# Cross-attention and feed-forward layer on one core: the front ordered anew, first statistics of two batches on VectorE, row scales on GpSimd

## The chip, the cores and the metric

The kernel runs on one core of one Trainium2 chip. The metric is the device time of one execution in microseconds (us), the median of three runs. Five instruction streams work side by side: TensorE (PE), VectorE (DVE), ScalarE (ACT), GpSimd (POOL) and SyncE (SP), which here issues the transfers. Each runs its own list in order; they meet only through semaphores.

## The reference

`x` is 4 batches of 512 tokens with 512 features. Two layers follow each other:

```python
x = x + xattn(layernorm(x), fside, ctx)      # per batch b
x = x + ffn(layernorm(x), gate_w, w1, b1, w2, b2)

def smooth_quant_linear(x, w):               # twice per batch: c = 1 with fside, c = 2 with ctx
    s = sqrt(max(amax(|x|, axis=0), EPS) / max(amax(|w|, axis=0), EPS))
    xs, ws = x / s, w * s
    x_scale = max(rowmax(|xs|), EPS) / 127
    w_scale = max(rowmax(|ws|), EPS) / 127
    return round(xs / x_scale) @ round(ws / w_scale).T * x_scale * w_scale.T

def xattn(x, w1, w2):
    gate, up = split(smooth_quant_linear(x, w1))
    return smooth_quant_linear(silu(gate) * up, w2)

def ffn(x, ...):                             # 2048 tokens together
    logits = x @ gate_w.T                    # 8 experts
    sel = top_k(logits.sum(over tokens), 2)  # two experts for all tokens
    rw = softmax(logits[:, sel])
    return sum_k rw_k * (gelu(x @ w1[sel_k] + b1[sel_k]) @ w2[sel_k] + b2[sel_k])
```

Which two experts are taken is known only when all tokens of all four batches are normalised for the second time. So no weight of an expert can be loaded before the front is nearly done.

## The kernel before, in words

The program has two parts. The **front** (everything up to the choice of the experts) works on four batches b = 0 to 3, each through two quantised products c = 1 and 2. The **main part** runs 16 pairs of 256 hidden features (the function `pair`, the first of them `first_pair`) through TensorE and is left as it is but for one router product and the place of some semaphore increments.

A batch goes through the front like this; the names are those of the code. `moments` gives mean and variance of its tokens; `inv_std` on GpSimd gives the inverse deviation; `normalise` on ScalarE writes the normalised batch; `normed` on TensorE transposes it into PSUM, and `amax_x` on VectorE takes the largest values of the columns (`raw_weight` and `amax_w`, `raw_context` and `amax_c` do it for the weights). `ratio_x`, `root` and `inverse` make the smoothing vector, `smooth_rows` spreads it over rows, `smooth_x` and `smooth_weight` multiply with it. Then come the **scales of rows**: the maximum of each row (`abs_max`), a clip and a factor (`scale`, one small tensor_scalar, 128x4), and a reciprocal (`rscale`); before the change `row_scales` did all three on VectorE. `round_x` (ScalarE) and `round_weight` (GpSimd) round with them, TensorE transposes the rounded values (`rounded_x`, `rounded_w`), ScalarE casts them to bf16 (`integers_x`, `integers_w`), TensorE multiplies (`product`), and VectorE multiplies the scales back in (`dequant`). Between the products stand `gate`, `gate_up_product` and `ratio_a`. After the second product `add_residual` updates `res`, and the second normalisation (`moments(b, 2)`, `inv_std(b, 2)`, `normalise(b, 2)`, `normed2`) feeds the router: `token_sums`, `token_total`, `expert_sums`, `choose_experts`, then the load of the first expert weights.

Nothing orders this work but five lists of calls, written out by hand, one for each engine, and the table `SLOT_USES`, which says in which order four PSUM slots of two banks are used. A TensorE step that fills a slot waits until the step before it in that slot's list is drained. A wait placed early in a list holds all that stands behind it on that engine.

At the start SP issues the transfers in this order: the gate weights, the biases, x0, x1, w0, x2, w1, x3, w2, w3 and then the four contexts (x and w are 1 MB each, a context is 0.5 MB). VectorE's first real work is `amax_w(0, 0)`; the first moments of all four batches are ScalarE's, the second ones VectorE's.

## Time and profile before

| | us |
|---|---|
| median of the runs | 832.31 (three runs: 832.25, 832.31, 834.96) |
| the profiled execution | 837.12 |
| its span, first to last instruction | 835.3 |
| TensorE busy | 776.2 (93%) |
| VectorE busy | 494.4 (59%) |
| GpSimd busy | 437.3 (52%) |
| ScalarE busy | 363.1 (43%) |

The profile's first page gives these sums for the whole span. Since front and main part differ, the stretches have to be read apart: in the first 160 us VectorE is the fullest engine, after it TensorE is. The granted clock of TensorE was 0.97 of full on average. Times of single instructions come from the one profiled execution, which took 4.8 us more than the median of the unprofiled runs.

### The profile page before, as it was taken

To read this page: it belongs to the slowest core of one execution; us is meant where nothing else is said; L and a number is where in the kernel's file an instruction comes from. 1 tells how busy PE (TensorE), PEld (TensorE's weight loads), DVE (VectorE), ACT (ScalarE), POOL (GpSimd) and SP (SyncE) were. 2 spreads that over 40 slices of the span, in tenths; PEclk is the share of its full clock that TensorE was granted. 3 is DMA by queue.
4 is the path that set the end of the run, shared out by engine and by line. 5 is a ranking of instruction groups with operands and counts; after the bars stand their busy time and mean duration, and the time that the engine had idled before them with its cause. 6 is when DMAs were issued, how large, how long until landed. Compare 5 with 4: busy or idle time off the path is not lost.

```text
span 835.3 us, 11356 instructions
## 1 busy us (share of the span) xinstructions
PE 776.2 (93%) x3577; PEld 627.6 (75%) x3577; DVE 494.4 (59%) x699; ACT 363.1 (43%) x682; POOL 437.3 (52%) x453
## 2 busy tenths in 40 slices
PE   3587775699999999999999999999999999999998
PEld 3476553478788888888888888888888888888886
DVE  2899998879764545454545454545454545454545
ACT  7965666845533333333333343434343424342422
POOL 1467887155655555555555555545454546364622
PEclk9889898699999999999999999999999999999999
DMA  8500000120101010101010101000000000000022
GB/s 337 171 1 1 0 1 1 51 75 1 51 1 51 1 51 0 50 0 51 0 50 2 49 12 38 22 28 25 25 25 25 25 25 25 25 25 25 0 92 111
DMA packets 19078, 32.35 MB, mean 39 GB/s; under 512 B 872, under 2 KB 11240, under 8 KB 18160
## 3 DMA queue, kind: packets, MB, share of 16 engines
q1 hardware_dynamic: 19056, 32.07, 10.8%
q8 instruction: 12, 0.20, 0.1%
q14 instruction: 10, 0.08, 0.0%
HBM read 27.87 MB, written 4.19 MB: 38 GB/s over the span
## 4 chain that ended last, share of the span: by engine, by line
PE 81%; DVE 12%; issue 2%; DMA 2%; ACT 1%; POOL 1%; SPq 0%; DVEq 0%; POOLq 0%; ACTq 0%
PE slot L746 41%; PE slot L733 33%; DVE rmax L1154 3%; PE slot L791 3%; DVE xf L1204 2%; DMA wv<-in_fside_BxS2xS 2%; DVE peak_x L1154 2%; DVE xf L1217 1%; PE slot L607 1%; DVE wv L1217 1%; DVE stats L1145 1%; PE slot L596 1%; DVE scale L1195 1%; POOL h_lo L416 1%; DVE peak_a L1154 1%
## 5 line engine op out<-in xcount | busy, mean ns | idle before, releaser
L733 PE MATMUL slot<-xo,a_hi 128*128 128x512 f32 x840 | 258.9, 389 | 0.0
L1445 DVE SCALAR_TENSOR_TENSOR res<-slot,rw,res 128x512 f32<-128x512 f32 x256 | 179.5, 750 | 131.1 <-PE slot L746 130.2
L1474 DVE TENSOR_TENSOR e<-slot,e 128x512 f32<-128x512 f32 x150 | 103.8, 692 | 171.7 <-PE slot L733 171.7
L746 PE MATMUL slot<-w_hi,h_hi 128*128 128x512 f32 x512 | 201.1, 393 | 0.4 <-POOL h_lo L416 0.4
L746 PE MATMUL slot<-w_lo,h_hi 128*128 128x512 f32 x512 | 199.5, 390 | 0.0
L746 PE MATMUL slot<-w_hi,h_lo 128*128 128x512 f32 x512 | 199.2, 389 | 0.0
L733 PEld LDWEIGHTS slot<-xo,a_hi 128*128 128x128 f32 x840 | 157.3, 188 | 33.4 <-DVE e L1474 0.2
L416 POOL TENSOR_TENSOR h_lo<-e,h_hi 128x512 fp32r<-128x512 f32 x96 | 138.0, 1450 | 57.2 <-ACT e L1030 56.2
L733 PE MATMUL slot<-xo,a_lo 128*128 128x512 f32 x420 | 163.5, 389 | 0.0
L746 PEld LDWEIGHTS slot<-w_hi,h_hi 128*128 128x128 f32 x512 | 96.1, 188 | 25.3 <-POOL h_lo L416 5.6
L746 PEld LDWEIGHTS slot<-w_hi,h_lo 128*128 128x128 f32 x512 | 96.1, 188 | 20.2
L746 PEld LDWEIGHTS slot<-w_lo,h_hi 128*128 128x128 f32 x512 | 96.1, 188 | 19.4
L416 POOL TENSOR_TENSOR h_lo<-hid,h_hi 128x512 fp32r<-128x512 f32 x32 | 44.1, 1379 | 123.5 <-ACT hid L1030 123.5
L733 PEld LDWEIGHTS slot<-xo,a_lo 128*128 128x128 f32 x420 | 78.8, 188 | 16.6
L1029 ACT ACTIVATE h_hi<-e,b_now 128x512 fp32r<-128x512 f32 x90 | 64.9, 722 | 58.1 <-DVE e L1474 57.7
L1070 ACT COPY e<-slot 128x512 f32<-128x512 f32 x30 | 17.6, 586 | 164.5 <-PE slot L733 164.5
L430 POOL TENSOR_TENSOR a_lo<-raw,a_hi 128x256 fp32r<-128x256 f32 x45 | 34.3, 762 | 96.0 <-ACT a_hi L923 96.0
L926 ACT CAST w_hi<-raw 128x512 fp32r<-128x512 f32 x32 | 19.8, 622 | 110.0 <-PE slot L746 110.0
L435 POOL TENSOR_TENSOR w_lo<-raw,w_hi 128x512 fp32r<-128x512 f32 x30 | 38.7, 1290 | 50.5 <-ACT w_hi L926 50.5
L1030 ACT ACTIVATE e<-e,b_now 128x512 f32<-128x512 f32 x90 | 63.8, 708 | 0.0
L1029 ACT ACTIVATE h_hi<-slot,b_now 128x512 fp32r<-128x512 f32 x38 | 26.2, 689 | 67.8 <-PE slot L733 56.6
L430 POOL TENSOR_TENSOR a_lo<-ssum,a_hi 128x256 fp32r<-128x256 f32 x60 | 43.9, 741 | 0.0
(144 smaller groups left out, 834.1 us busy)
## 6 DMA issues: line engine op xcount, KB each, us to landing
raw<-in_L_ffn_w SPq DMA_DIRECT2D x32, 512.0 KB, 3.3
res<-in_x SPq DMA_DIRECT2D x4, 1024.0 KB, 9.7
wv<-in_fside_BxS2xS SPq DMA_DIRECT2D x4, 1024.0 KB, 14.9
out_x<-res SPq DMA_DIRECT2D x3, 1024.0 KB, 3.9
cv<-in_ctx SPq DMA_DIRECT2D x4, 512.0 KB, 11.0
out_x<-res SPq DMA_DIRECT2D x4, 256.0 KB, 2.7
b_row<-in_L_ffn_b SPq DMA_DIRECT2D x2, 256.0 KB, 4.3
b_rows<-in_L_ffn_b SPq DMA_DIRECT2D x1, 64.0 KB, 1.9
```

Source lines behind the costliest of these rows:

```text
L416: g.tensor_tensor(h_lo[:, i, :], hid[i][:, :], h_hi[:, i, :].bitcast(F32), ALU.subtract).then_inc(h_ready, 1)
L430: g.tensor_tensor(a_lo[:, i, :, :], A_OF[i], a_hi[:, i, :, :].bitcast(F32), ALU.subtract).then_inc(a_ops_ready, 1)
L435: g.tensor_tensor(w2_lo[:, f, :], raw2[:, f, :], w2_hi[:, f, :].bitcast(F32), ALU.subtract).then_inc(w2_ready, 1)
L733: last = t.matmul(dst, a[:, i, k, :], xo[tp][:, v, k, :], start=(start and n == 0), stop=(n == 3 * H - 1), skip_group_check=True)
L746: last = t.matmul(y_bank[j][:, :], a[:, i, j * P:(j + 1) * P], v[:, f, :], start=(start and n == 0), stop=(not start and n == 2), skip_gro ...
L791: last = t.matmul(TILE_BANK[n], a[:, 2 * f + h, k, :], xo[q][:, v, k, :], start=(m == 0), stop=(m == 3 * KD - 1))
L926: s.copy(w2_hi[:, f, :], raw2[:, f, :]).then_inc(w2_hi_ready, 1)
L1029: s.activation(h_hi[:, i, :], src, ACT.Gelu_apprx_tanh, bias=bias).then_inc(hid_ready, 1)
L1030: s.activation(hid[i][:, :], src, ACT.Gelu_apprx_tanh, bias=bias).then_inc(hid_ready, 1)
L1154: return v.tensor_reduce(dst, src, AX.X, ALU.max, apply_absolute_value=True)
L1445: v.scalar_tensor_tensor(out=r, in0=y_bank[j][:, :], scalar=rw[:, ds(p, 1), n:n + 1].rearrange("p a b -> p (a b)"), in1=r, op0=ALU.mult, o ...
L1474: v.tensor_tensor(dst[:, :], src, other[:, :], ALU.add).then_inc(comb_ready, 1)
```

## The change

- SP issues the transfers in the order x0, w0, x1, w1, c0, x2, w2, c1, x3, w3, c2, c3. The gate weights and biases are issued by ScalarE.
- The first moments of batches 0 and 1 go to VectorE, ahead of and between its first maxima. Those of batches 2 and 3 stay on ScalarE.
- The second moments of batch 0 go from VectorE to ScalarE. The second normalisation of batch 2 goes from ScalarE to GpSimd.
- `row_scales` is split in three: `row_max` on VectorE, `row_scale` on GpSimd (the small tensor_scalar, 16 in all), `row_inverse` on VectorE, which waits for GpSimd. The three stand at different places of their lists, with other work between them.
- All five lists and `SLOT_USES` are written in a new order. The router products stand as 0, sums, 1, 2, 3, with none left inside the first pair; before they stood as sums, 0, 1, 2, and the fourth after the first tile of the first pair.

```diff
-            sp.dma_start(gw_rows, gate_w).then_inc(gw_load, 16)
-            sp.dma_start(b1_rows[:, :], b1_v).then_inc(b1_load, 16)
...
             load_x(0)
+            load_w(0)
             load_x(1)
-            load_w(0)
+            load_w(1)
+            load_c(0)
             load_x(2)
-            load_w(1)
+            load_w(2)
+            load_c(1)
             load_x(3)
-            load_w(2)
             load_w(3)
...
+            def row_scale(b, c, w):
+                pool.wait_ge(rmax_done, ROW_MAXIMA.index("xw"[w] + f"{c}.{b}") + 1)
+                g.tensor_scalar(scale[b][:, w, :], rmax[b][:, w, :], QEPS, 1.0 / QMAX, ALU.max, ALU.mult
+                                ).then_inc(scale_done, 1)
+
...
+            def normalise(b):
+                pool.wait_ge(nmr_ready[b], 2)
+                for j in range(TT):
+                    g.tensor_scalar(xv[b][:, j, :], res[:, b * TT + j, :], rstd[1][b][:, j:j + 1], nmr[1][b][:, j:j + 1],
+                                    ALU.mult, ALU.add).then_inc(xn2_ready[b], 1)
...
+            router(0)
             expert_sums()
-            router(0)
             router(1)
             router(2)
+            router(3)
...
-                    if tp == 0:
-                        router(3)
...
-            def row_scales(b, m, w, ready):
-                link(abs_max(rmax[b][:, w, :], m))
-                link(v.tensor_scalar(scale[b][:, w, :], rmax[b][:, w, :], QEPS, 1.0 / QMAX, ALU.max, ALU.mult))
-                v.reciprocal(rscale[b][:, w, :], scale[b][:, w, :]).then_inc(ready[b], 1)
+            def row_max(b, m, w):
+                abs_max(rmax[b][:, w, :], m).then_inc(rmax_done, 1)
+
+            def row_inverse(b, c, w):
+                dve.wait_ge(scale_done, SCALES.index("xw"[w] + f"{c}.{b}") + 1)
+                v.reciprocal(rscale[b][:, w, :], scale[b][:, w, :]).then_inc((xscale_ready, wscale_ready)[w][b], 1)
```

The two places where the order matters most for what follows. First VectorE at the very start; peak_x0 are the column maxima of batch 0 (its input and its weight), stats1 the first statistics of batch 1. Before:

```order
L1154 TENSOR_REDUCE peak_x0<-slot3 128x2
L1154 TENSOR_REDUCE peak_x0<-slot2 128x2
L1154 TENSOR_REDUCE peak_x1<-slot2 128x2
L1154 TENSOR_REDUCE peak_x1<-slot3 128x2
L1154 TENSOR_REDUCE peak_x0<-slot3 128x2
L1154 TENSOR_REDUCE peak_x0<-slot2 128x2
L1169 TENSOR_SCALAR clip0<-peak_x0 128x8
```

The same place now, up to the same clip0:

```order
L1183 BN_STATS stats0<-res 128x6 x4
L1186 BN_AGGR mv0<-stats0 128x2 x4
L1192 TENSOR_REDUCE peak_x0<-slot0 128x2
L1183 BN_STATS stats1<-res 128x6 x4
L1186 BN_AGGR mv1<-stats1 128x2 x4
L1188 TENSOR_SCALAR nmean1_1<-mv1 128x4
L1189 TENSOR_SCALAR var_e1_1<-mv1 128x4
L1192 TENSOR_REDUCE peak_x0<-slot2 128x2
L1192 TENSOR_REDUCE peak_x0<-slot0 128x2
L1192 TENSOR_REDUCE peak_x1<-slot1 128x2
...
L1207 TENSOR_SCALAR clip0<-peak_x0 128x8
```

Two statistics have moved in between the same six maxima; both wait for a transfer of x. The second place is GpSimd's list in the first product; wv0 is the weight of batch 0, multiplied with its smoothing row (L342 before, L348 now) and rounded (L348 before, L354 now). Before:

```order
L342 TENSOR_TENSOR wv0<-wv0,xf0 128x512 x4
L327 TENSOR_TENSOR rstd1_2<-var_e1_2,neg_half 128x4
L330 TENSOR_TENSOR nmr1_2<-nmean1_2,rstd1_2 128x4
L336 TENSOR_TENSOR sroot1<-ratio1,half 128x4
L348 TENSOR_SCALAR wv0<-wv0,rscale0 128x512 x4
L342 TENSOR_TENSOR wv1<-wv1,xf0 128x512 x4
L336 TENSOR_TENSOR sroot2<-ratio2,half 128x4
L348 TENSOR_SCALAR wv1<-wv1,rscale1 128x512 x4
```

Now:

```order
L348 TENSOR_TENSOR wv0<-wv0,xf0 128x512 x4
L359 TENSOR_SCALAR scale0<-rmax0 128x4
L333 TENSOR_TENSOR rstd1_3<-var_e1_3,neg_half 128x4
L336 TENSOR_TENSOR nmr1_3<-nmean1_3,rstd1_3 128x4
L359 TENSOR_SCALAR scale0<-rmax0 128x4
L354 TENSOR_SCALAR wv0<-wv0,rscale0 128x512 x4
L348 TENSOR_TENSOR wv1<-wv1,xf0 128x512 x4
L342 TENSOR_TENSOR sroot2<-ratio2,half 128x4
L359 TENSOR_SCALAR scale1<-rmax1 128x4
L348 TENSOR_TENSOR wv2<-wv2,xf0 128x512 x4
L359 TENSOR_SCALAR scale1<-rmax1 128x4
L354 TENSOR_SCALAR wv1<-wv1,rscale1 128x512 x4
```

Each small scale stands between the large pieces and behind four of them in two cases, and the rounding that waits for it stands later in the same list.

## Rows read from the trace of the kernel before

**Rows 1.** The page: the chain that ended last, shares by engine

```profile
PE 81%; DVE 12%; issue 2%; DMA 2%; ACT 1%; POOL 1%; SPq 0%; DVEq 0%; POOLq 0%; ACTq 0%
```

**Rows 2.** Who TensorE waited for, from 168 to 300 us: total, times, longest

```profile
PE slot L746 <- POOL h_lo L416: 0.4, 1, 0.4
```

**Rows 3.** Stretches: length, each engine's busy time (x instructions), PEclk, DMA share, GB/s

```profile
120.00:130.00 10.00, 5.59 (x37) 4.61 (x36) 6.41 (x14) 8.68 (x18) 4.99 (x9) 0.84 0.00 1
140.00:150.00 10.00, 2.99 (x20) 2.04 (x20) 9.90 (x18) 7.20 (x14) 6.30 (x5) 0.87 0.01 2
150.00:160.00 10.00, 7.14 (x32) 5.66 (x32) 7.68 (x16) 7.89 (x16) 2.40 (x4) 0.61 0.00 0
260.00:300.00 40.00, 40.00 (x177) 32.84 (x176) 20.23 (x28) 14.82 (x28) 21.25 (x21) 1.00 0.08 27
```

**Rows 4.** Stretches, VectorE alone: length, busy (x instructions), PEclk, DMA share, GB/s

```profile
0.00:26.30 26.30, 7.93 (x10) 1.00 0.93 345
26.30:142.60 116.30, 109.48 (x167) 0.85 0.04 14
142.60:161.90 19.30, 16.83 (x35) 0.71 0.00 1
```

**Rows 5.** Timeline of the start: start, length, engine, line [idle before <-releaser]

```profile
0.74 0.41 SPq L251 DMA_DIRECT2D wsc_row<-in_L_ffn_gate_w  x1
1.63 0.89 SPq L255 DMA_DIRECT2D res<-in_x  x2
6.92 0.63 ACT L846 ACTIVATE xf<-res 128x512 f32<-128x512 f32 x1 [3.98 <-DMA res<-in_x]
12.61 3.65 PE L508 MATMUL slot<-ident,wv 128*128 128x128 f32 x16 [8.94 <-DMA wv<-in_fside_BxS2xS]
17.72 3.63 PE L508 MATMUL slot<-ident,wv 128*128 128x128 f32 x16 [1.46 <-DMA wv<-in_fside_BxS2xS]
28.30 3.46 DVE L1154 TENSOR_REDUCE peak_x<-slot 128x2 f32<-128x1024 f32 x3
```

**Rows 6.** Timeline, VectorE: one `moments` of four pieces, first and last row

```profile
111.18 2.46 DVE L1145 BATCH_NORM_STATS2 stats<-res 128x6 f32<-128x512 f32 x4
114.16 0.16 DVE L1151 TENSOR_SCALAR var_e<-mv 128x4 f32<-128x4 f32 x1
```

**Rows 7.** Groups, 0 to 170 us: busy us, mean ns of one, idle before

```profile
L1195 DVE TENSOR_SCALAR scale<-rmax 128x4 f32<-128x4 f32 x16 | 7.4, 462 | 0.6
```

**Rows 8.** VectorE's scale operation: ns min/median/max

```profile
L1195 DVE TENSOR_SCALAR scale<-rmax x16: 170/281/1843, 38.7 to 132.8; 128x4 f32<-128x4 f32 x16
```

**Rows 9.** Groups of GpSimd, 0 to 160 us: busy us, mean ns, idle before

```profile
L342 POOL TENSOR_TENSOR wv<-wv,xf 128x512 f32<-128x512 f32 x16 | 19.9, 1281 | 5.5 <-ACT xf L865 5.5
L348 POOL TENSOR_SCALAR wv<-wv,rscale 128x512 f32<-128x512 f32 x16 | 10.8, 693 | 6.7 <-DVE rscale L1196 6.7
L327 POOL TENSOR_TENSOR rstd<-var_e,neg_half 128x4 f32<-128x4 f32 x8 | 9.0, 1126 | 25.1 <-ACT var_e L854 18.6 <-DVE var_e L1151 6.6
L348 POOL TENSOR_SCALAR cv<-cv,rscale 128x256 f32<-128x256 f32 x16 | 7.4, 482 | 1.3 <-DVE rscale L1196 1.3
```

**Rows 10.** Timeline of the tail, TensorE, VectorE and ScalarE

```profile
142.60 3.32 DVE L1264 TENSOR_TENSOR res<-res,wv 128x512 f32<-128x512 f32 x2
142.62 1.97 PE L596 MATMUL slot<-ident,xf 128*128 128x128 f32 x16 [1.57 <-DVE wv L1217]
151.36 7.17 PE L596 MATMUL slot<-ident,xf 128*128 128x128 f32 x32 [6.77 <-ACT xf L833]
161.06 7.26 PE L607 MATMUL slot<-xo,gwt 128*16 128x512 f32 x24
161.73 0.16 DVE L1283 FIND_INDEX8 top_i<-top_v,sum_row 128x8 uint32<-128x8 f32 x1
166.56 1.32 ACT L920 CAST a_hi<-raw 128x256 fp32r<-128x256 f32 x4
168.16 0.62 PE L791 MATMUL slot<-xo,a_hi 128*128 128x512 f32 x2
```

More of the change, by code:

```diff
@@ L366, in _ @@
             root(0, 1)
+            root(1, 1)
+            inv_std(2, 1)
+            smooth_weight(0, 1)
+            row_scale(0, 1, 0)
             inv_std(3, 1)
-            smooth_weight(0, 1)
-            inv_std(2, 1)
-            root(1, 1)
+            row_scale(0, 1, 1)
             round_weight(0, 1)
@@ L1325, in _ @@
             dve.sem_inc(y_free, TT)
+            dve.sem_inc(comb_ready, 15)
+            dve.sem_inc(h_ready, 4)
+            moments(0, 1)
             amax_w(0, 0)
+            moments(1, 1)
             amax_w(0, 1)
+            amax_x(0, 0)
             amax_w(1, 0)
+            amax_x(0, 1)
             amax_w(1, 1)
[L1330 to L1331 removed]
             ratio_x(0)
@@ L1334, in _ @@
             inverse(0, 1)
-            amax_w(2, 0)
-            amax_w(3, 0)
             amax_x(1, 1)
             ratio_x(1)
+            amax_c(0)
             smooth_x(0, 1)
+            inverse(1, 1)
+            scale_x(0, 1)
+            amax_w(3, 0)
+            amax_w(2, 0)
             scale_w(0, 1)
+            amax_w(3, 1)
+            row_inverse(0, 1, 1)
+            row_inverse(0, 1, 0)
             amax_w(2, 1)
-            amax_w(3, 1)
-            inverse(1, 1)
-            amax_c(1)
+            smooth_x(1, 1)
@@ L1345, in _ @@
             amax_x(2, 0)
-            amax_c(0)
-            smooth_x(1, 1)
             amax_x(2, 1)
             ratio_x(2)
+            scale_x(1, 1)
+            inverse(2, 1)
+            amax_x(3, 0)
             scale_w(1, 1)
+            amax_x(3, 1)
+            row_inverse(1, 1, 0)
+            smooth_x(2, 1)
+            ratio_x(3)
+            row_inverse(1, 1, 1)
+            scale_w(2, 1)
             dequant(0, 1, 0)
-            inverse(2, 1)
+            scale_x(2, 1)
+            inverse(3, 1)
@@ L1353, in _ @@
             dequant(0, 1, 1)
-            amax_x(3, 0)
-            smooth_x(2, 1)
-            amax_x(3, 1)
-            ratio_x(3)
-            scale_w(2, 1)
-            ratio_a(0)
-            inverse(3, 1)
-            dequant(1, 1, 0)
-            inverse(0, 2)
-            dequant(1, 1, 1)
-            smooth_x(3, 1)
-            smooth_x(0, 2)
-            scale_w(0, 2)
-            scale_w(3, 1)
-            ratio_a(1)
+            row_inverse(2, 1, 0)
+            row_inverse(2, 1, 1)
@@ L1369, in _ @@
+            amax_c(1)
+            smooth_x(3, 1)
+            scale_x(3, 1)
+            dequant(1, 1, 0)
+            ratio_a(0)
+            dequant(1, 1, 1)
+            scale_w(3, 1)
+            row_inverse(3, 1, 0)
+            amax_c(2)
+            row_inverse(3, 1, 1)
+            inverse(0, 2)
             dequant(2, 1, 0)
             dequant(2, 1, 1)
+            smooth_x(0, 2)
+            ratio_a(1)
+            scale_x(0, 2)
+            scale_w(0, 2)
             inverse(1, 2)
-            amax_c(2)
+            row_inverse(0, 2, 0)
@@ L1373, in _ @@
+            amax_c(3)
+            row_inverse(0, 2, 1)
+            dequant(3, 1, 0)
             smooth_x(1, 2)
-            dequant(0, 2, 0)
-            scale_w(1, 2)
-            dequant(0, 2, 1)
-            dequant(3, 1, 0)
             ratio_a(2)
             dequant(3, 1, 1)
-            moments(0, 2)
-            inverse(2, 2)
-            dequant(1, 2, 0)
-            amax_c(3)
-            smooth_x(2, 2)
-            scale_w(2, 2)
-            ratio_a(3)
-            inverse(3, 2)
+            scale_x(1, 2)
@@ new lines, in _ @@
+            scale_w(1, 2)
+            row_inverse(1, 2, 0)
+            dequant(0, 2, 0)
+            row_inverse(1, 2, 1)
+            inverse(2, 2)
+            ratio_a(3)
+            smooth_x(2, 2)
+            scale_x(2, 2)
+            inverse(3, 2)
+            row_inverse(2, 2, 0)
+            dequant(0, 2, 1)
+            scale_w(2, 2)
+            smooth_x(3, 2)
+            scale_x(3, 2)
+            row_inverse(2, 2, 1)
+            dequant(1, 2, 0)
+            scale_w(3, 2)
+            row_inverse(3, 2, 0)
@@ L1388, in _ @@
             dequant(1, 2, 1)
-            smooth_x(3, 2)
-            scale_w(3, 2)
+            row_inverse(3, 2, 1)
             dequant(2, 2, 0)
+            dequant(2, 2, 1)
             moments(1, 2)
-            dequant(2, 2, 1)
             dequant(3, 2, 0)
             dequant(3, 2, 1)
+            moments(2, 2)
             add_last_residual()
-            moments(2, 2)
             moments(3, 2)
             keep_lo(0, 0)
+            keep_lo(1, 0)
             normalise_last()
+            token_sums(2)
```

290 lines of the change are left out of this document (156 added, 134 removed), and 16 rows, old and new, of the table SLOT_USES.

## The prediction

> **What bounds the kernel now.** I read the chain that ended last first: TensorE holds 81% of it [rows 1]. Then I asked who TensorE waits for once the main part runs: from 168 to 300 us there is a single wait of 0.4 us [rows 2], and the stretch 260 to 300 is busy for 40.00 of 40 us [rows 3]. So from its first tile, at 168.16 us [rows 10], TensorE runs without a gap. The main part is hardly changed and can't get shorter. What the change is worth is by how much earlier that stream starts, plus what is taken out of it.
>
> In the front the reader is to see VectorE. From the clip of batch 0 (26.30) to the end of the last `dequant`, where the last residual starts (142.60 [rows 10]), it is busy for 109.5 of 116.3 us; before that for 7.9 of 26.3 us, behind it for 16.8 of 19.3 us [rows 4]. It is the full engine of the middle; in the first 26 us it waits for transfers and transposes; behind 142.60 a chain runs over four engines up to the choice of the experts at 161.73 [rows 10]. I take the four stretches one by one.
>
> **A, the start, up to the clip of batch 0: 26.30 before.** x0 is there at 6.92, w0 at 12.61, w1 at 17.72 [rows 5]. The step from 6.92 to 12.61 is x1 and w0, 5.7 us. In the new order w0 and x1 follow x0, so x1 lands where w0 did, at 12.6. SP no longer issues two small loads first, which took 0.9 us (0.74 to 1.63 [rows 5]); they now run beside the large ones, so I count 0.6 of it: 12.0. VectorE then needs one `moments`, 111.18 to 114.32, 3.1 us [rows 6], and five of the six maxima, 3.46/3 = 1.15 each [rows 5], 5.8 us. The other `moments` and the first maximum fit between x0 and x1. The clip comes at 12.0 + 3.1 + 5.8 = 20.9. A is 5.4 us shorter, and two `moments`, 6.1 us of new VectorE work lie in time that was idle. Bounds: if x1 came only at 14.8, one transfer of half that 5.7 later, the gain is 26.30 - 23.7 = 2.6; with the full 0.9 and no gap, 6.2.
>
> **B, the middle, 116.3 us before.** Removed from VectorE: 16 scale operations, 7.4 us [rows 7]; the median is 281 ns and the longest 1843 [rows 8], and the long ones stood beside GpSimd's work. Each also had a link on either side, for which I estimate 0.1 us, 1.6 in all. The second moments of batch 0 leave too: 3.1 [rows 6]. Together 12.1 us. Added to GpSimd: 16 tensor_scalars of 128x4, which the trace does not show there. Its tensor_scalar took 693 ns with 512 elements and 482 with 256 [rows 9], which leaves 0.27 for almost none; the upper end is its power on 128x4, 1.13 us [rows 9]. I take 0.27, since the operation is of the first kind: 4.3 us. If GpSimd stood in the way with all of it at 1.13, it were 18.
>
> What hides these 4.3 us is VectorE's other work between `row_max` and `row_inverse`: in the first product a maximum of 1.15 us or more stands there. Queued behind a waiting `row_inverse` on VectorE are `dequant` and `smooth_x`; ScalarE's and GpSimd's rounding waits for it. In the second product the cover is thin: maxima are half as long, GpSimd has the weights of ctx, the gated products and the residuals to do, and `scale_w` of batches 2 and 3 waits for it. I laid the new lists out in time, every instruction starting when its list and its semaphores let it, with its duration from the rows. VectorE's larger waits there are 1.0 us before a `dequant(3,1)`, 1.2 before the row maxima of the ctx weight of batch 2, 2.1 before `dequant(2,2)` and 0.5 twice elsewhere; with small ones 8.0 us, against the 6.8 that it idles now (116.30 - 109.48 [rows 4], more than half of it in 120 to 130 [rows 3]). In it the two small operations of the moments of batch 1 also stand 2.5 us behind GpSimd's residuals. So of the 12.1 us the 1.6 of links were idle anyway; busy time falls by 10.5 - 2.5 = 8.0, idle time rises by 1.2, and B comes out 6.8, say 7 us, shorter. The old lists, laid out in the same way, come within 1.1 us of the trace at 160 us, so I trust the layout to 2 or 3 us. Bounds: 0, if the waits eat everything, and 12.1, if none is added.
>
> A rule speaks against B. The Trainium skill (SBUF — State Buffer, "SBUF: two separate sides") says that VectorE and GpSimd share a port pair as an exclusive lock: a VectorE operation with two SBUF inputs or in a fast mode, and a GpSimd operation, block each other whole; Perfetto Trace Analysis, "Optimizing Scalar/DVE Operations", adds that moving work between those two might not help. By that rule the trace agrees as to the lock: the same 128x4 operation takes 170 to 1843 ns [rows 8]. The rule would leave the 16 operations their own 0.27 us on GpSimd but take VectorE's wait for the lock away, so it does not decide against the sum; what would is the first rival.
>
> **C, the tail, 19.3 us before.** Each tail has the same chain: residual, moments, inverse deviation, normalise, transposes, token sums. GpSimd normalises batch 2 with four tensor_scalars of 0.69 [rows 9], 2.8 us, and ScalarE spent 2.9 on it. One router product more now stands ahead of the sums. TensorE ran the first 16 transposes there in 1.97 us and the last 32 in 7.17 [rows 10], 0.12 against 0.22 each: its granted clock was 0.61 of full in 150 to 160, that is mostly the lower level of 1.2 GHz, after a stretch with 3 of 10 us busy [rows 3]. At that level eight router matmuls (24 took 7.26 [rows 10], 0.30 each) can delay the sums by up to 2.4; at the full one the layout hides them. I take C 1.5 longer; bounds 1 shorter and 5 longer.
>
> **D, from the choice to the dense stream, 6.4 us.** SyncE, the load, ScalarE's and VectorE's split of the weights stay; the router products 1, 2, 3 fill the time that 0, 1, 2 filled, so nothing moves. But the fourth product no longer stands in the dense stream: eight matmuls of 512 columns at 40.00/177 = 0.226 [rows 3], 1.8 us. Bounds 0 and 1.8.
>
> **The sum**: -5.4 - 7.0 + 1.5 - 1.8 = -12.7 us. The profiled execution took 837.12 us (span 835.3), so it would take 824.4; against the median of 832.31 it is **819.6 us**.
>
> **The rivals.** *First, GpSimd becomes the bound of the middle.* For it: in the second product it already holds most of its time, and 4.3 us come to it. Against: in 120 to 130 it was busy for 5.0 of 10 us [rows 3], and 12.1 us leave VectorE. B gives nothing: -5.4 + 1.5 - 1.8 = -5.7, 826.6 us.
>
> *Second, slower: the small scales queue behind GpSimd's large pieces.* The place is `row_scale` behind `smooth_weight` (four pieces of 1.28, 5.1 us [rows 9]), with `row_inverse` and all of VectorE standing behind it. For each of 16 scales w us of VectorE's time are lost beyond the layout; the point from which the kernel is slower by 4.2 is 16 w = 12.7 + 4.2, w = 1.06 us. With two pieces each (2.56) in half of the cases it is 20.5 us, 840.1 us. For it: VectorE is in order and the two engines are the fullest. Against: the scales stand ahead of the next large group in most places, and VectorE has 1.2 us or more to do meanwhile.
>
> *Third, the clock stays low through the tail.* 64 transposes of the second normalisation at 0.22 instead of 0.12 cost 6.4 us, of which the 32 that already ran so [rows 10] are in the time before: 3.2 more, 822.8 us. For it: TensorE is no busier in the new tail.
>
> *Fourth, the transfers don't come earlier* (A gives 2.6): 822.4 us. *Fifth, no waits are added in the middle*: B gives 12.1, 814.5 us. That the change does not do what it says has no room here: the operations are gone from VectorE's list.
>
> **How the numbers follow.** Forecast 0.50, GpSimd bound 0.13, scales queue 0.04, low clock 0.14, late transfers 0.09, no waits 0.10. The range runs from the fifth rival (814.5) to the first (826.6), 814 to 827; what it leaves out is the slower rival and some of each end. Half a per cent, 4.2 us, is about what a measurement of this kernel can tell from no change; faster means below 828.1. The forecast, the last three rivals (0.83) and half of the first are faster, 0.89; the other half, with a layout that was too kind by a few us, is the same, 0.07; slower 0.04.
>
> **What would show it.** A: the clip of batch 0 at 20.9 us and x1 landing near 12. B: the line of the scales on GpSimd at 0.27 us each and gone from VectorE, VectorE's last `dequant` ended near 130. C: the choice of the experts near 151 (161.73 - 10.9). D: TensorE's first tile near 157, no router product inside the first pair. The prediction is wrong if a scale on GpSimd takes about 1 us, if VectorE waits for `scale_done` for more than a few us in total, or if TensorE shows gaps behind its first tile.

## The result, and the profile after

| | median us | runs | lowest to highest |
|---|---|---|---|
| before | 833.26 | 4 | 832.25 to 834.96 |
| changed | 824.26 | 4 | 822.56 to 826.86 |

The ratio is 0.989 (95%: 0.986 to 0.993): 9.0 us faster, where 12.7 were forecast (819.6, range 814 to 827). Further runs, made beside the experiments below, give 835.3 to 835.8 for the kernel before (17, 23 and 11 runs in three groups) and 825.94 for the changed one (6 runs, beside the first group): 9.4 us there. One of the 23, at 867.68 us and a granted clock of 0.878, is a slow execution and left out of the ratios. I take the difference of the medians as 9.4.

The profiled execution of the changed kernel took 823.26 us (span 821.4). The main part first: the chain that ended last is again TensorE's (shares by engine).

```profile
PE 82%; DVE 9%; POOL 4%; issue 3%; DMA 1%; ACT 1%; ACTq 0%; DVEq 0%; POOLq 0%
```

VectorE's share fell by three points and GpSimd's rose by as many [rows 1]. Who TensorE waits for, from 150 to 300 us (total, times, longest):

```profile
PE slot L781 <- POOL h_lo L450: 0.4, 1, 0.4
PE slot L826 <- issue: 0.3, 1, 0.3
PE slot L641 <- DVE xo L1268: 0.2, 1, 0.2
```

As before [rows 2] there is nothing to gain there. From the first matmul with `w_hi` to the end the two spans have 653.1 and 653.0 us left, so the whole difference is made ahead of it. The stretches of VectorE by the same three moments as [rows 4] (length, then busy time of PE, PEld, DVE, ACT and POOL, granted clock, DMA share, GB/s):

```profile
0.00:21.44 21.44, 12.15 (x69) 10.10 (x69) 13.46 (x31) 8.52 (x14) 3.51 (x15) 1.00 0.94 347
21.44:130.59 109.15, 80.54 (x506) 59.67 (x512) 99.64 (x142) 82.17 (x161) 90.60 (x125) 0.90 0.08 30
130.59:150.13 19.54, 16.12 (x67) 11.02 (x68) 17.30 (x35) 14.27 (x28) 10.11 (x10) 0.57 0.00 1
```

The reader is to see three things. The start is 4.9 us shorter, and VectorE does 5.5 us more work in it. The middle is 7.1 shorter (116.26 to 109.15): VectorE's busy time falls by 9.8, and its idle time grows from 6.8 to 9.5. The tail, counted from the end of the last `dequant` (142.56 before) to the choice (161.73), is 0.4 longer, 19.5 against 19.2, and TensorE's granted clock in it is 0.57 of full. The start, in rows that answer to [rows 5] (start, length, engine, line):

```profile
1.36 0.36 ACTq L965 DMA_DIRECT2D b_rows<-in_L_ffn_b  x1
7.25 0.47 PE L523 MATMUL slot<-ident,b_rows 128*128 128x128 f32 x1 [3.40 <-DMA b_rows<-in_L_ffn_b]
8.39 2.46 DVE L1183 BATCH_NORM_STATS2 stats<-res 128x6 f32<-128x512 f32 x4
9.03 3.65 PE L542 MATMUL slot<-ident,wv 128*128 128x128 f32 x16 [1.31 <-DMA wv<-in_fside_BxS2xS]
12.58 2.46 DVE L1183 BATCH_NORM_STATS2 stats<-res 128x6 f32<-128x512 f32 x4
21.44 0.16 DVE L1207 TENSOR_SCALAR clip<-peak_x 128x8 f32<-128x8 f32 x1
```

Moving the two small loads to ScalarE's queue freed SyncE's, and x0 landed at 5.66 us and x1 at 11.40. But the biases came only at 7.2, and VectorE's first statistics stand behind the copy of what they feed, so they began at 8.39 though x0 had been there for 2.7 us. The groups of the scales (busy us, mean ns, idle before), where [rows 7] had 7.4 us on VectorE:

```profile
L359 POOL TENSOR_SCALAR scale<-rmax 128x4 f32<-128x4 f32 x16 | 3.7, 233 | 7.8 <-DVE rmax L1192 6.8
L1236 DVE RECIPROCAL rscale<-scale 128x4 f32<-128x4 f32 x16 | 2.5, 167 | 0.6 <-POOL scale L359 0.5
```

A scale costs GpSimd 233 ns, and VectorE waits for all sixteen for 0.5 us in total. VectorE's longer waits in the middle (21.4 to 130.6):

```profile
DVE wv L1260 <- PE slot L609: 3.4, 1, 3.4
DVE rmax L1192 <- POOL cv L348: 2.0, 2, 1.4
DVE xf L1249 <- ACT xf L901: 1.0, 1, 1.0
```

The wait of 1.4 is for the ctx weight of batch 2, the place that the prediction named with 1.2. The end of the middle and the tail, in time, from the timelines of all engines:

```profile
119.72 2.73 DVE L1260 SCALAR_TENSOR_TENSOR wv<-slot,scale,wsc_row 128x512 f32<-128x512 f32 x4 [3.40 <-PE slot L609]
121.74 7.42 POOL L373 TENSOR_TENSOR res<-res,wv 128x512 f32<-128x512 f32 x6
125.43 1.31 DVE L1188 TENSOR_SCALAR nmean<-mv 128x4 f32<-128x4 f32 x1
126.65 1.31 DVE L1189 TENSOR_SCALAR var_e<-mv 128x4 f32<-128x4 f32 x1
135.52 4.09 POOL L378 TENSOR_SCALAR xf<-res,rstd,nmr 128x512 f32<-128x512 f32 x4
137.84 2.85 DVE L1268 TENSOR_TENSOR xo<-xf,xo 128x1024 fp32r<-128x1024 f32 x2
139.58 1.97 POOL L333 TENSOR_TENSOR rstd<-var_e,neg_half 128x4 f32<-128x4 f32 x1
142.82 3.87 PE L630 MATMUL slot<-ident,xf 128*128 128x128 f32 x16 [0.76 <-ACT xf L866]
146.34 2.48 PE L641 MATMUL slot<-xo,gwt 128*16 128x512 f32 x8
150.13 0.16 DVE L1326 FIND_INDEX8 top_i<-top_v,sum_row 128x8 uint32<-128x8 f32 x1
156.04 0.70 PE L826 MATMUL slot<-xo,a_hi 128*128 128x512 f32 x2 [0.26 <-issue]
```

The two small operations of the moments take 1.31 us each beside GpSimd's six residual additions; elsewhere they take 0.16 [rows 6]. GpSimd's four pieces of `normalise` take 4.09 us where I counted 2.8 (three take 0.77 and the last, beside `keep_lo`, 1.84), and its power 1.97 where the mean was 1.13 [rows 9]: the last piece and the power overlap VectorE's `keep_lo` (L1268), a subtraction of two SBUF operands. By the rule of the Trainium skill (SBUF — State Buffer, "SBUF: two separate sides") VectorE and GpSimd lock each other out there; the trace agrees, with these 1.84 and 1.97 us as the price for GpSimd.

### The profile page after: what moved, and what is told of

Read it like the earlier page. It is cut to its first block, busy times and chain, and to the rows that moved or that the text cites. A ratio compares the mean times of both kernels' runs of the same rounds, so it can differ in the third digit from the quotient of the medians.

```text
span 821.4 us, 11341 instructions
## 1 busy us (share of the span) xinstructions
PE 775.2 (94%) x3570; PEld 624.4 (76%) x3577; DVE 487.6 (59%) x693; ACT 355.2 (43%) x660; POOL 445.9 (54%) x473
## 4 chain that ended last, share of the span: by engine, by line
PE 82%; DVE 9%; POOL 4%; issue 3%; DMA 1%; ACT 1%; ACTq 0%; DVEq 0%; POOLq 0%
PE slot L781 42%; PE slot L768 34%; PE slot L826 3%; DVE rmax L1192 2%; DVE xf L1249 1%; DVE peak_x L1192 1%; POOL res L373 1%; DVE peak_a L1192 1%; DVE xf L1260 1%; DMA b_rows<-in_L_ffn_b 1%; POOL cv L348 1%; DVE stats L1183 1%; POOL rstd L333 1%; POOL h_lo L450 1%; PE slot L563 1%
## 5 line engine op out<-in xcount | busy, mean ns | idle before, releaser
L768 PEld LDWEIGHTS slot<-xo,a_hi 128*128 128x128 f32 x840 | 157.3, 188 | 33.4 <-DVE e L1542 0.2
L781 PEld LDWEIGHTS slot<-w_lo,h_hi 128*128 128x128 f32 x512 | 96.1, 188 | 19.5
## 6 DMA issues: line engine op xcount, KB each, us to landing
wv<-in_fside_BxS2xS SPq DMA_DIRECT2D x4, 1024.0 KB, 12.7
```

Of the source, the lines that this page charges most:

```text
L768: last = t.matmul(dst, a[:, i, k, :], xo[tp][:, v, k, :], start=(start and n == 0), stop=(n == 3 * H - 1), skip_group_check=True)
L781: last = t.matmul(y_bank[j][:, :], a[:, i, j * P:(j + 1) * P], v[:, f, :], start=(start and n == 0), stop=(not start and n == 2), skip_gro ...
```

## The experiments

Each kernel is compared with runs of the kernel before on the same chip in the same minutes, and the ratios are to these. Their median is 835.3 us beside the first four that follow here (changed again, new lists with the scales on VectorE, new lists with the old transfers, router product back), 835.8 beside the next four (before again, old lists with the scales on GpSimd, old lists with the new transfers, small loads on SyncE) and 835.4 beside the last four. Where a difference to the changed kernel is given, it is to its repetition, 825.94, which ran beside the first group only. How far such differences can be trusted is seen from two sets of one program: the kernel before gave 833.76 as an experiment (12 runs) and 835.8 beside it (23 runs), and the changed kernel 824.26 and 825.94. A difference of about 2 us between two kernels is therefore not told from this scatter by its median alone. Moments are read from each trace: the clip of batch 0, the end of the last `dequant`, the choice of the experts, TensorE's first tile with `a_hi`.

| kernel | median us | ratio to before, 95% | clip | dequant | choice | tile |
|---|---|---|---|---|---|---|
| before, again | 833.76 | 0.998, 0.996 to 1.000 | 25.6 | 141.3 | 158.7 | 164.6 |
| changed, again | 825.94 | 0.989, 0.986 to 0.992 | 21.3 | 132.4 | 152.5 | 158.4 |
| new lists, scales on VectorE | 828.23 | 0.992, 0.989 to 0.994 | 21.8 | 137.5 | 157.3 | 163.2 |
| new lists, old transfers | 833.59 | 0.998, 0.996 to 0.999 | 24.1 | 142.8 | 163.0 | 168.9 |
| router product back | 827.88 | 0.992, 0.989 to 0.994 | 21.6 | 132.4 | 151.5 | 157.3 |
| old lists, scales on GpSimd | 848.28 | 1.015, 1.013 to 1.017 | 26.1 | 155.7 | 173.1 | 179.1 |
| old lists, new transfers | 836.26 | 1.001, 0.999 to 1.003 | 24.6 | 143.4 | 160.8 | 166.8 |
| small loads on SyncE | 826.16 | 0.988, 0.986 to 0.990 | 22.0 | 132.7 | 153.0 | 158.9 |
| statistics on ScalarE | 829.26 | 0.992, 0.990 to 0.994 | 26.9 | 136.0 | 155.0 | 160.9 |
| filler transposes | 824.56 | 0.987, 0.984 to 0.989 | 22.2 | 131.5 | 150.3 | 155.9 |
| tail reordered | 823.44 | 0.985, 0.982 to 0.987 | 21.9 | 131.5 | 150.5 | 156.2 |
| filler and reordered | 824.97 | 0.987, 0.985 to 0.989 | 21.6 | 133.6 | 152.6 | 158.3 |

**The changed kernel once more.** No edit.

> The changed kernel once more, unaltered: the control of the other three, and a second trace of the same program. If the executions of one program differ by where TensorE's clock falls in the front (theory), its first dense tile will not start at 156.0 us as in the first trace but up to 2 us off, with other stretches at the lower clock, and the main part will take the same 665 us. If they differ in the main part instead (rival), the first tile starts within 0.3 us of 156.0 and the end moves. Time 822 to 827.

825.94 us (824.53 to 827.1). The trace differs from the first one by 2.3 us at the first tile and by 0.0 from the first matmul with `w_hi` on (653.01 and 653.03). More than half of the difference, 1.3 us, comes at one place of the middle (about 0.5 lies ahead of it and 0.5 in the tail):

```profile
125.94 3.76 DVE L1188 TENSOR_SCALAR nmean<-mv 128x4 f32<-128x4 f32 x1
129.68 2.71 DVE L1260 SCALAR_TENSOR_TENSOR wv<-slot,scale,wsc_row 128x512 f32<-128x512 f32 x4
```

The operation of 0.16 us took 3.76 here, and `dequant` behind it began 1.8 us later than in the first trace. GpSimd at that time, same trace:

```profile
122.25 7.43 POOL L373 TENSOR_TENSOR res<-res,wv 128x512 f32<-128x512 f32 x6
129.85 1.02 POOL L333 TENSOR_TENSOR rstd<-var_e,neg_half 128x4 f32<-128x4 f32 x1 [0.17 <-DVE var_e L1189]
```

The small operation ended when the six additions of 1.24 us each ended: it stood behind three of them in a row. In the first trace it began just as far into the six additions (3.69 us after their start in both) and took 1.31, as the operation behind it did. What decides between the two cases is not shown. Of the nine traces with the new lists and the scales on GpSimd three show the long wait.

**The scales back on VectorE, new lists kept.**

```diff
-                abs_max(rmax[b][:, w, :], m).then_inc(rmax_done, 1)
+                link(abs_max(rmax[b][:, w, :], m))
+                v.tensor_scalar(scale[b][:, w, :], rmax[b][:, w, :], QEPS, 1.0 / QMAX, ALU.max, ALU.mult
+                                ).then_inc(scale_done, 1)
```

and GpSimd's 16 `row_scale` calls go.

> The changed kernel with the 16 scale operations back on VectorE, each straight behind its row maximum with a wait in between; all five lists otherwise as they are, GpSimd's 16 operations gone. Theory (VectorE sets the pace of the middle, and the operation costs it its own time, two links and the wait for the port that GpSimd holds): laid out in time the last dequant ends 6.6 us later and the first dense tile starts 6.7 us later: 830 to 832. Rival (the new order did it, the place of the scales is nothing, since they fit in waits): within 2 us of the changed kernel.

828.23: 2.3 us over the repetition of the changed kernel, less than I expected. The two sets do not overlap (827.67 to 831.4 against 824.53 to 827.1), but 2.3 us is hardly more than the scatter between sets of one program. Its profiled execution was the slowest of its runs (831.4), so the 5 us that its trace shows in the middle are too many. The operation itself:

```profile
L1212 DVE TENSOR_SCALAR scale<-rmax 128x4 f32<-128x4 f32 x16 | 9.2, 577 | 0.6
```

9.2 us leave VectorE when the scales go to GpSimd, and about 2.3 of them reach the end. The rest is lost on the way, in waits by my reading; no run separates them.

**The old transfers under the new lists.** Again small loads first on SyncE, then x0 x1 w0 x2 w1 x3 w2 w3 and ctx last.

```diff
+            sp.dma_start(gw_rows, gate_w).then_inc(gw_load, 16)
+            sp.dma_start(b1_rows[:, :], b1_v).then_inc(b1_load, 16)
-            load_w(0)
             load_x(1)
+            load_w(0)
...
-            act.dma_start(gw_rows, gate_w).then_inc(gw_load, 16)
-            act.dma_start(b1_rows[:, :], b1_v).then_inc(b1_load, 16)
```

> The changed kernel with the transfers in the old order (x0, x1, w0, x2, w1, x3, w2, w3, contexts) and the two small loads on SyncE in front of them again. Theory (stretch A is set by when w0, x1 and w1 land and carried to the end by a full VectorE): clip of batch 0 at about 23.3 instead of 21.4, and since w1 and the contexts come later than the new lists want them, the last dequant 6.6 us and the first dense tile 6.7 us later: 829 to 832. Rival (the start has slack; transfers are hidden anyway): under 2 us.

833.59: 7.7 us over the changed kernel, more than forecast. The clip is only 2.7 us later; the rest is lost behind it, where VectorE's list still asks for tiles in the order in which the new transfers would bring them. Who VectorE waits for, 0 to 143 us (the 4.1, the 3.6 and the 2.7 lie ahead of the clip, the 5.9 behind it, for the transposes of a normalised batch):

```profile
DVE peak_x L1190 <- PE slot L559: 5.9, 1, 5.9
DVE peak_x L1190 <- PE slot L542: 4.4, 2, 4.1
DVE gwt L1159 <- PE slot L523: 3.6, 1, 3.6
DVE stats L1181 <- DMA res<-in_x: 2.7, 1, 2.7
```

**The fourth router product back in the dense stream.**

```diff
-            router(3)
...
+                    if tp == 0:
+                        router(3)
```

> The changed kernel with the fourth router product and its copy back inside the first pair, behind the first tile. Theory: the first tile starts where it did (within 0.3 us), and the eight matmuls of 0.23 us come into the dense stream: 1.9 us slower. Rival (the wait for the first expert weights had no room, so taking the product out lets the first tile start sooner): no difference.

827.88, 1.9 us over the changed kernel, as expected by the median. The chain of waits of this kernel shows the product at its old place (start, length, what):

```profile
157.34 4.57 PE slot L825 x12
161.91 1.84 PE slot L641 x8
163.75 2.72 PE slot L825 x12
```

The product takes 1.84 us of the stream. But that is not all that this trace shows. Twelve matmuls ahead of it take 4.57 us and the twelve behind it 2.72: TensorE had idled 2.5 us before the first tile, and its granted clock from 157.3 to 162.0 us is 0.64. From the first tile to the first matmul with `w_hi` this kernel needs 15.8 us against 12.3, so 3.4 more, and its first tile is 1.0 us earlier than in the repetition. That the medians differ by just the price of the product is in part luck.

**The kernel before once more.** No edit.

> The kernel before, unaltered, for a second trace of it. Theory (the main part from the first down product takes 653.0 us in every execution, and what differs between executions of one program is the front, by where TensorE's clock falls): main part within 0.2 us of 653.1, the middle from the first clip to the last dequant 1 to 3 us shorter than the 116.3 of the first trace, since that execution was at the slow end of its runs. Rival: the same front, another main part.

833.76 (832.34 to 837.13). Its trace, from a run of 834.97, is nearer to the median than the one that I predicted from (837.12): its tail has the length 17.4 us instead of 19.2, at a granted clock of 0.80 instead of 0.71. Two things that I expected did not come: the middle is only 0.6 us shorter than in the first trace (1 to 3 expected), and from the first matmul with `w_hi` on it takes 654.4 us, not 653.1. TensorE's part of that is the same within 0.2 us; from the end of its last matmul to the end of the span it is 5.1 us against 3.9, and no engine works at its end: the last transfer of the output lands later. Its last transposes and its router products, to be held against 7.17 and 7.26 [rows 10]:

```profile
149.15 6.32 PE L596 MATMUL slot<-ident,xf 128*128 128x128 f32 x32 [5.84 <-ACT xf L833]
158.00 5.72 PE L607 MATMUL slot<-xo,gwt 128*16 128x512 f32 x24
```

VectorE's middle in this trace and in the repetition of the changed kernel (columns as above), and the sixteen scales in this one, to be held against 7.4 us [rows 7]:

```profile
25.64:141.29 115.65, 83.35 (x507) 63.15 (x512) 107.36 (x166) 78.54 (x146) 87.77 (x110) 0.85 0.05 16
21.32:132.40 111.08, 83.43 (x513) 59.35 (x512) 101.13 (x142) 83.47 (x163) 91.69 (x126) 0.88 0.08 30
L1195 DVE TENSOR_SCALAR scale<-rmax 128x4 f32<-128x4 f32 x16 | 6.0, 375 | 0.5
```

**The scales on GpSimd with the old lists.** On the kernel before: each `row_scale` stands behind the `smooth_weight` of its batch, the maxima and inverses stay where they are.

```diff
-                link(abs_max(rmax[b][:, w, :], m))
-                link(v.tensor_scalar(scale[b][:, w, :], rmax[b][:, w, :], QEPS, 1.0 / QMAX, ALU.max, ALU.mult))
+                abs_max(rmax[b][:, w, :], m).then_inc(rmax_done, 1)
+                scales[0] += 1
+                dve.wait_ge(scale_done, scales[0])
```

> The kernel before with nothing changed but the 16 scale operations: they are GpSimd's, behind the weight products of the same batch, and VectorE waits for each in place, its lists not rearranged. Theory (the move pays only because the new lists put other work between row maximum and inverse; in place, VectorE stands behind up to four products of 1.28 us): laid out in time the last dequant ends 8 to 9 us later and the first tile 7 to 9 us later, 842 to 845. Rival (the move itself is the gain): 2 to 7 us faster than before.

848.28, 12.5 us slower than before (ratio 1.015). VectorE's waits in the middle of this kernel, 26 to 155 us:

```profile
DVE rscale L1224 <- POOL scale L357: 8.5, 16, 1.5
DVE peak_a L1179 <- PE slot L609: 5.5, 2, 3.4
DVE xf L1232 <- ACT xf L890: 2.1, 3, 1.3
DVE smooth L1215 <- POOL sroot L340: 2.1, 1, 2.1
```

VectorE's busy time in the middle is 107.16 us against 109.48 [rows 4] and 107.36 in the second trace of before, but the stretch is 129.5 long against 116.3 and 115.7. Every one of the sixteen inverses waits for GpSimd, 0.53 us on average, and what follows each of them is late for TensorE and ScalarE. This is the mechanism of the second rival. At 0.53 us for each scale it costs half of what I had set as the point from which the changed kernel would be slower; here that is enough, since no reordered list gives anything back. So the move as placed here does not pay without the new lists, in which VectorE has a maximum or a `smooth_x` to do between a row maximum and its inverse. Only one placing in GpSimd's old list was run, behind the weight products; whether the scales ahead of these products would cost less was not tested. The Trainium skill (Perfetto Trace Analysis, "Optimizing Scalar/DVE Operations") says that moving work between these two engines might not help, because they share a port. The time agrees for the move alone; the waits above are for the moved operation itself, so they do not show that reason.

**The new transfers under the old lists.** On the kernel before, x0 w0 x1 w1 c0 x2 w2 c1 x3 w3 c2 c3; the small loads stay on SyncE.

```diff
             load_x(0)
-            load_x(1)
             load_w(0)
-            load_x(2)
+            load_x(1)
             load_w(1)
+            load_c(0)
+            load_x(2)
```

> The kernel before with nothing changed but the order of the large transfers, which is the new one (x0, w0, x1, w1, c0, x2, ...). Theory (transfers, moments and lists belong together: the first clip comes 0 to 1 us sooner since it stands behind ScalarE's two moments and w1, and batches 2 and 3 get their data later than the old lists want it): 0 to 3 us slower than before. Rival (the transfer order alone is stretch A's gain): 3 to 5 us faster, first clip near 22.

836.26 against 835.8: no difference (0.999 to 1.003). The clip is 1 to 1.7 us earlier than in the traces of before, and the gain is gone by the end of the `dequant`.

**The two small loads back on SyncE, ahead of the large ones.**

```diff
+            sp.dma_start(gw_rows, gate_w).then_inc(gw_load, 16)
+            sp.dma_start(b1_rows[:, :], b1_v).then_inc(b1_load, 16)
...
-            act.dma_start(gw_rows, gate_w).then_inc(gw_load, 16)
-            act.dma_start(b1_rows[:, :], b1_v).then_inc(b1_load, 16)
```

> The changed kernel with the gate weights and biases issued by SyncE in front of the large loads, as before, the new order of the large ones kept. In the changed kernel the biases landed at 7.2 us (3.2 before), and VectorE's first statistics, which stand behind them, began at 8.4 with x0 there at 5.7. Theory: they begin at about 6.9 now (x0 lands 0.9 us later), but the first clip hangs on x1 and w1 as well and comes 0 to 0.8 us sooner: 0 to 1 us faster than the changed kernel. Rival (the late biases cost the whole 1.5 us to the end): 1.5 us faster.

826.16, the same as the changed kernel. VectorE's start in this kernel:

```profile
6.64 2.48 DVE L1183 BATCH_NORM_STATS2 stats<-res 128x6 f32<-128x512 f32 x4 [2.29 <-DMA res<-in_x]
12.12 1.22 DVE L1192 TENSOR_REDUCE peak_x<-slot 128x2 f32<-128x1024 f32 x1 [2.32 <-PE slot L544]
```

The first statistics begin 1.7 us earlier than in the changed kernel, and the first maximum then waits 2.3 us for the transposes of w0, which is late by the small loads. Either order of the queues costs the same: mending the late biases in this way gains nothing.

**The first statistics of batches 0 and 1 on ScalarE again.** They are those of the first normalisation.

```diff
+            moments(0, 1)
+            moments(1, 1)
```

in ScalarE's list ahead of `normalise(0, 1)`, and gone from VectorE's.

> The changed kernel with the first moments of batches 0 and 1 back on ScalarE, ahead of its two first normalisations; transfers and all else as changed. Theory (stretch A: ScalarE needs 5.8 us for each of the two, one behind the other, and the first clip waits for them): laid out in time the first clip comes at 26.0 instead of 21.6 and the first dense tile 4.2 us later, 4 to 5 us slower than the changed kernel, about 830. Rival (the middle has slack that takes it up): under 2 us.

829.26, 3.3 us over the changed kernel, a little less than forecast. The clip comes at 26.9 us, 5.5 us later; at the end of the last `dequant` 3.6 to 5.4 of it are left (136.0 against 132.4 and 130.6).

**Filler transposes against the low clock.** 30, 12 and 12 transposes of the identity into a free bank, ahead of the last three batches of the second normalisation.

```diff
+            def busy_work(n):
+                emptied("y.0.0")
+                for _ in range(n):
+                    t.transpose(slot[0][:, 1, 0:P], ident[:, :], ident[:, :])
...
+                if h == 0 and b:
+                    busy_work((30, 12, 12)[b - 1])
```

> The changed kernel with 30, 12 and 12 transposes more on TensorE (of the identity into a bank that nobody uses then) ahead of the second normalisation's transposes of batches 1, 2 and 3, where TensorE idled 5.2, 1.7 and 0.8 us. They do nothing but keep TensorE at work. Theory (the tail is 2.7 us longer than the old one in good part because TensorE runs 14 to 17 us of it at the lower clock, after it has idled): the stretch from 130 to 147 shows the full clock, the last 16 transposes take 2.0 instead of 3.9 us, the choice of the experts comes 2 to 3 us sooner: 2 to 3 us faster than the changed kernel. Rival (the clock falls all the same, or the tail hangs on VectorE and GpSimd and not on TensorE): no gain, or up to 3 us slower for the added work.

824.56: 1.4 us under the repetition of the changed kernel and 0.3 over its first set (824.26), so no difference is shown. The stretch of the tail in the changed kernel (length, busy time of PE, PEld, DVE, ACT and POOL, granted clock, DMA share, GB/s):

```profile
130.00:140.00 10.00, 6.75 (x24) 4.06 (x25) 9.86 (x25) 6.41 (x13) 8.87 (x11) 0.51 0.01 2
```

The same stretch with the filler, and the first router product behind the last transposes, from this kernel's timeline:

```profile
130.00:140.00 10.00, 6.17 (x43) 4.33 (x41) 9.86 (x27) 6.29 (x13) 8.89 (x11) 1.00 0.00 0
146.21 2.02 PE L648 MATMUL slot<-xo,gwt 128*16 128x512 f32 x8
```

With the filler TensorE is at its full level of 2.4 GHz from 130 us to the first tile (1.00 instead of 0.51 in this stretch), and that router product takes 2.02 us instead of 2.48. Yet the tail is 18.7 us long against 19.5 and 20.1. By these traces the low clock costs about a microsecond there: up to 142.8 us the chain that ends last is VectorE's and GpSimd's, but for one ScalarE operation.

**The tail reordered on VectorE.** VectorE's part of the last normalisation goes ahead of two of the splits `keep_lo`, and the token sums of batch 2 ahead of one.

```diff
-            keep_lo(0, 0)
-            keep_lo(1, 0)
             normalise_last()
+            keep_lo(0, 0)
             token_sums(2)
             keep_lo(0, 1)
+            keep_lo(1, 0)
             keep_lo(1, 1)
```

> The changed kernel with the two subtractions for the low parts of batches 0 and 1 that stood between the last moments and the last normalisation on VectorE put behind the latter. In both traces of the changed kernel they held GpSimd's last two steps up: its normalisation piece took 1.84 us instead of 0.77 and the power behind it 1.97 instead of 1.01. Theory (this port conflict is 1 to 2 us of the longer tail): var_e to the last nmr takes 2.0 us instead of 3.9; part of it is lost again since the subtractions come later: laid out, 0 to 1.1 us faster. Rival (nothing of it reaches the end): same.

823.44 (822.19 to 824.17), 2.5 us under the repetition of the changed kernel and 0.8 under its first set, 0.985 of the time before: the lowest median of all. The trace shows less: its tail is 19.0 us against 19.5 and 20.1, so 0.5 to 1.1 us come from the reordered tail. It has the long wait of 3.76 us in the middle too, and its first tile (156.21) is no earlier than in the first trace of the changed kernel (156.04). Where the rest of the 2.5 comes from is open. GpSimd's part of the tail in this kernel, to be held against 4.09 and 1.97 above:

```profile
136.41 3.05 POOL L378 TENSOR_SCALAR xf<-res,rstd,nmr 128x512 f32<-128x512 f32 x4
139.43 1.00 POOL L333 TENSOR_TENSOR rstd<-var_e,neg_half 128x4 f32<-128x4 f32 x1
140.51 0.20 POOL L336 TENSOR_TENSOR nmr<-nmean,rstd 128x4 f32<-128x4 f32 x1
```

With no VectorE operation on two SBUF operands beside them, the four pieces take 1.0 us less and the power its usual 1.0.

**Both.** The filler and the reordered tail.

> Both of the last two edits. Theory: they add up, 2 to 4 us faster than the changed kernel, 822 to 824. Rival: the router products and the load of the first expert weights set the first tile, and all that is won before the choice is lost behind it: the same as the better of the two.

824.97: the two do not add up. The trace has the small operation's delay in the middle again (`dequant` ends at 133.6), and a tail of 19.0 us, as with the reordering alone. Whether the filler itself costs something in the middle stays open; the intervals of these last kernels overlap.

## Why the prediction was right in kind and 3.3 us too good

The sum by its four terms, once from the two traces first shown, and once from the two traces nearest to the medians (before again, 834.97 us; changed again, 825.67):

| term | forecast | first pair | pair near the medians |
|---|---|---|---|
| A, start to the clip | -5.4 | -4.9 | -4.3 |
| B, clip to the last `dequant` | -7.0 | -7.1 | -4.6 |
| C, to the choice | +1.5 | +0.4 | +2.7 |
| D, to the first tile | 0 | -0.5 | -0.1 |
| D, router product and the rest behind the tile | -1.8 | -1.9 | -3.2 |
| sum | -12.7 | -14.0 | -9.5 |

**The bound was read rightly.** TensorE's stream is as long as before but for the router product, and everything moved with its start. No gap came behind the first tile but the 0.4 us that stood there before. Between the traces nearest to the medians the three terms of the front come to 6.2 us, where the forecast had 10.9; the last row hides a part of that.

**A** held, 0.5 to 1.1 us short. x1 landed at 11.4, as worked out (12.0). What I had not seen is that the biases, now in ScalarE's queue, would land 4 us later than before, and that VectorE's first statistics stand behind them. The small loads put back on SyncE's queue give nothing. The two statistics moved into the idle start were worth 3.3 us by themselves.

**B is the term that fell shortest of the medians**: 4.6 us, where 7.0 were forecast. Its working is there. In the first pair VectorE's busy time fell by 9.8 us (8.0 forecast) and its idle time rose by 2.7 (1.2), the scale takes 233 ns on GpSimd (270), and two of the named waits are there, for the ctx weight 1.4 us, and behind GpSimd's residuals, where the two small operations take 2.3 more than alone. The other wait of 3.4 us, for `dequant(2,2)` behind TensorE, is longer than the 2.1 laid out. Between the traces near the medians, though, busy time fell by only 6.2 us, and idle time rose by 1.7. Two terms that I set as fixed vary between executions. The sixteen scales cost 7.4 us in the trace that I predicted from and 6.0 in the second trace of the same program (7.7 with the old lists and new transfers). And the wait of the two small operations behind GpSimd, set at 2.5 us, is 2.3 or 3.6 between two runs of one program. Together that is about the 2.4 us that are missing; smaller differences go both ways. It is not one place alone: with the router product back both small operations took 1.31 us and the middle was still 110.8 us long.

**C** ran short by 1.2 us against the medians. The layout had the tail from 19.3 up by 1.5, that is 20.8. The new tail is 19.0 to 20.3 us in the traces with the new lists (18.7 with the filler), so it came out 0.5 to 1.8 shorter than laid out. What was mis-sized more is the tail before: three of four traces with the old lists have one of 17.4 us, and the trace that I predicted from had 19.2, in an execution at the slow end of its kernel. Of these 1.8 us, 0.9 are the last residual on VectorE (3.32 us [rows 10] against 2.38) and 0.9 the last 32 transposes (7.17 against 6.32).

**The yardstick** joins B and C: I took the difference to an execution of 837.12 us and set it against a median of 832.31. The tail of 19.2 us was that execution's own, and its scales cost 1.4 us more than in the second trace of the same program. The first pair sets it against an execution of 823.26, below the median of its kernel; that B agrees with the forecast to 0.1 us in it is in part luck.

**D** held in the product: it takes 1.84 us of the stream where it is put back (1.8 forecast), and from the first tile to the first matmul with `w_hi` the changed kernel needs 12.3 us against 14.1. In the pair near the medians the row shows 3.2, of which 1.4 lie behind the first matmul with `w_hi`, mostly in the last transfer of the output, which the change does not touch.

**The rivals.** Three of them gave a time nearer to the measured 824.26 than the forecast did: GpSimd as the bound of the middle (826.6), the low clock (822.8) and late transfers (822.4). None of the three mechanisms is there at its price. GpSimd is not the bound: B is 4.6 to 7.1 us and not nothing. Scales that queue behind large pieces are real, but only with the old lists: 12.5 us slower. The low clock was there (0.57 in the tail) and costs about 1 us by the filler's traces, not 3.2. Late transfers: refuted by the landing of x1 (11.4, not 14.8). No added waits: refuted, idle time rose by 1.7 to 2.7 us.

**The parts are not a sum.** Taken from the changed kernel one at a time, the transfers are worth 7.7 us, the statistics 3.3, the scales 2.3 and the router product 1.9, together 15 where the whole is 9.4. The last two are about as large as the scatter between sets of one program. Put alone into the kernel before, the transfers give 0 and the scales cost 12.5. The second moments of batch 0 on ScalarE, the second normalisation of batch 2 on GpSimd and the new order of the lists as such were never taken back alone, so their shares are not known. My four stretches did not need this, since they cut the time and not the change; a sum over edits would have gone wrong.

## What to carry to other kernels

When an operation goes to another in-order engine, what pays is the other work that stands between its issue and its use: the same 16 scales cost 12.5 us in place and gain about 2 with the lists reordered around them. Cut a prediction by stretches of time rather than by edits, and take the yardstick from an execution near the median: a trace at the slow end of its runs puts its own misfortune into the forecast. Look for small VectorE operations that stand beside a run of GpSimd's long ones, and for GpSimd chains beside VectorE's operations on two SBUF operands; moving two `keep_lo` behind the last normalisation took 1.0 us off GpSimd's four pieces and 1.0 off its power, at no cost that the runs show. And before a difference of 2 us is believed, see how far two sets of one program lie apart: here it was up to 2.0.

## What the runs showed of the hardware

- A VectorE operation of 128x4 (0.16 us alone) beside GpSimd's additions of 1.24 us can wait for three of them in a row and take 3.76 us; in another run of the same program it took 1.31.
- GpSimd pays too: one 128x512 tensor_scalar took 1.84 us beside VectorE's subtraction of two SBUF operands, against 0.77 for its neighbours, and its power on 128x4 took 1.97 us instead of 1.00.
- The scale of 128x4 took GpSimd 233 ns, and VectorE 375 and 462 ns on average in the two traces of the kernel before and 577 among the new lists: for this short operation GpSimd was the faster of the two as they ran here.
- A small load on ScalarE's queue, issued at 1.36 us beside 1 MB loads on SyncE's, was used only at 7.25; ahead of them on SyncE's queue it did not hold up the first statistics, which began at 6.64.
- Two traces of the changed kernel differed by 2.3 us at the first tile and by 0.02 us behind the first matmul with `w_hi`; two of the kernel before by 3.5 us at the first tile and by 1.3 us the other way behind it, nearly all of that after TensorE's last matmul. What differs between runs is the front, and at times the last transfer.
- Where TensorE had idled 2.5 us ahead of the dense stream, its granted clock was 0.64 over the next 4.7 us, and twelve matmuls took 4.57 us instead of 2.72.
